# Experts of a fused transformer kernel: three product banks, roots on GpSimd, a last end in halves, and one head fewer inside the causal stage

## The reference

```python
h = x + _gqa(_rmsnorm(x, attn_norm_w), wq, wk, wv, wo)   # causal, 16 heads of 8, 4 key/value heads
out = h + _moe(_rmsnorm(h, ffn_norm_w), gate_w, expert_w)
...
logits = t @ gate_w.T                       # 8 experts
w, sel = jax.lax.top_k(logits, TOP_K)       # TOP_K = 2
w = softmax(w)
for e in range(N_EXPERTS):
    out = out + comb[:, e, None] * (t @ expert_w[e].T)
```

## Time and profile before

| | us |
|---|---|
| median of 3 runs | 719.98 (717.72 to 722.4) |
| the profiled execution | 719.72 |
| its span, first to last instruction | 718.0 |

### The profile page before, as it was taken

The page is one execution under the profiler, slowest core; times in us unless marked ns, Lnnn a source line. Parts: engine busy times, 40 slices in busy tenths (PEclk is TensorE's granted clock), DMA queues, the critical chain, the costliest instruction groups (busy, mean ns, idle before and its releaser), DMA issues. The chain is left out here.

```text
span 718.0 us, 11711 instructions
## 1 busy us (share of the span) xinstructions
PE 559.0 (78%) x3810; PEld 309.0 (43%) x3810; DVE 524.0 (73%) x2256; ACT 367.5 (51%) x748; POOL 250.6 (35%) x414
## 2 busy tenths in 40 slices
PE   1966488478866999589999999999999978868660
PEld 1855487376654664112233333333334533535220
DVE  6699998532564776599899999999981554676883
ACT  5741145301102667004678778888787453655562
POOL 2001118600004568201344444444444443424443
PEclk9987565556986999655899999999999888988895
DMA  8000000000000283300111211112100000000001
GB/s 301 1 1 1 1 1 0 0 1 0 1 1 1 77 252 123 100 0 6 29 35 35 56 34 30 34 34 56 36 1 7 1 1 1 0 0 31 0 29 58
DMA packets 17003, 24.76 MB, mean 34 GB/s; under 512 B 3182, under 2 KB 13950, under 8 KB 16766
## 3 DMA queue, kind: packets, MB, share of 16 engines
q1 hardware_dynamic: 16366, 21.91, 9.9%
q10 hardware_dynamic: 576, 2.10, 0.8%
HBM read 13.65 MB, written 10.35 MB: 33 GB/s over the span
## 5 line engine op out<-in xcount | busy, mean ns | idle before, releaser
L1406 DVE CUSTOM_DVE_ANT_0 d_masked_S<-d_pS,d_wide_mask 128x512 bf16<-128x512 f32 (+3 forms) x512 | 217.0, 485 | 12.1 <-PE d_pS L1548 8.0
L1522 ACT ACTIVATE d_P<-d_pT 128x768 f32<-128x768 f32 (+1 forms) x192 | 166.0, 883 | 62.8 <-PE d_pT L1548 61.9
L1375 POOL TENSOR_SCALAR_AFFINE_SELECT d_P<-d_P 128x256 f32<-128x256 f32 x256 | 103.4, 417 | 174.9 <-ACT d_P L1522 174.9
L1548 PE MATMUL d_pS<-Ks,Qs 48*128 48x512 bf16 (+3 forms) x512 | 111.2, 332 | 23.7 <-DVE d_mx L1406 13.0
L1548 PE MATMUL d_pO<-d_P,V 128*32 128x512 f32 (+3 forms) x1024 | 98.6, 460 | 1.8 <-POOL d_P L1375 1.8
L1548 PE MATMUL d_pT<-Qs,Ks 51*128 51x512 bf16 (+3 forms) x512 | 73.1, 314 | 1.6 <-ACT d_mT L1492 1.6
L1548 PEld LDWEIGHTS d_pS<-Ks,Qs 48*128 48x128 bf16 x512 | 34.9, 97 | 77.3 <-DVE d_mx L1406 67.4
L1548 PEld LDWEIGHTS d_pT<-Qs,Ks 51*128 51x128 bf16 x512 | 20.8, 95 | 74.6 <-ACT d_P L1522 43.2
L1845 PE MATMUL e_PE<-gate_expT,w_qkvT 128*128 128x512 f32 x96 | 48.7, 655 | 4.3 <-PEq L58 2.5
L1406 DVE DVE_READ_ACCUMULATOR2_ANT d_mx<- 128x1 f32 x512 | 42.4, 83 | 0.0
L1548 PEld LDWEIGHTS d_pO<-d_P,V 128*32 128x32 f32 x1024 | 20.8, 109 | 32.9 <-issue 29.6
(11 more groups left out here) (309 smaller groups left out, 1059.2 us busy)
## 6 DMA issues: line engine op xcount, KB each, us to landing
Qs<-q_stack SPq DMA_DIRECT2D x32, 192.0 KB, 3.1
q_stack<-Qp SPq DMA_DIRECT2D x8, 384.0 KB, 2.6
X<-in_x_dram ACTq DMA_DIRECT2D x4, 512.0 KB, 6.1
q_stack<-Qp SPq DMA_DIRECT2D x8, 256.0 KB, 2.5
out_dram<-e_moe SPq DMA_DIRECT2D x4, 512.0 KB, 2.6
w_qkvT<-in_w_qkvT_dram SPq DMA_DIRECT2D x1, 1536.0 KB
Ks<-k_stack SPq DMA_DIRECT2D x32, 48.0 KB, 3.2
q_stack<-Qp SPq DMA_DIRECT2D x8, 128.0 KB, 2.1
```

What stands on the lines that cost most here:

```text
L1375: last = nc.gpsimd.affine_select(out=view, in_=view, compare_op=ALU.is_ge, fill=0.0, base=0, pattern=[[0, 2], [1, 128]], channel_multiplie ...
L1406: last = nc.vector.tensor_tensor_reduce(out=out_[:, at:at + w], in0=src[:, at:at + w], in1=wide_mask[:, 512 - w:512], scale=1.0, scalar=LO ...
L1522: nc.scalar.activation(P[pair % 4][:, :, P_AT[unit]:P_AT[unit] + w], pT[(3 * pair + unit) % 2][:, :, 0:w], ACT.Exp, scale=float(HD4) ** -0 ...
L1548: return nc.tensor.matmul(out, lhsT, rhs, start=start, stop=stop)
```

## The change

Inside the causal stage only chunk 0's head is left (`EARLY` = 1). The heads of chunks 1 to 3 lie in the experts' stage, where the steps now run from eight tiles ahead of a chunk to one ahead. PSUM is shared out anew: one PA tile instead of two, and three product banks instead of two; PE may write tile u once tile u - 3 has been scaled, and waits for the scaled logits of the head before ahead of the next head's transposes. Both roots of the experts' stage (RMS of a head, deviation of a chunk's end) move from ACT and DVE to POOL: a multiply-add and a power of -0.5, with `half_power` kept from the causal stage. POOL's list runs by turns, with each half-add one turn later. The last chunk's end is cut in halves of four tiles: DVE totals the first half at turn 30; after the last product the second half; ACT normalises the first half, DVE the second, DVE adds x to both, and each half has its own store.

```diff
-EARLY = 2
+EARLY = 1
...
-        PA = [ph.ps(f"PA{k}", [128, CT, D]) for k in two]
-        PE_ = [ph.ps(f"PE{k}", [128, NE, D]) for k in two]
+        PA = ph.ps("PA", [128, CT, D])
+        RING = 3
+        PE_ = [ph.ps(f"PE{k}", [128, NE, D]) for k in range(RING)]
+        LAST = CHUNKS - 1
+        HALF = CT // 2
+        scaled = lambda u: (sm["scaled_a" if u % 2 else "scaled_d"], u // 2 + 1)
...
-        PE_STEPS = {-11: "attention_by_channel", -9: "project", -7: "h_by_channel", -5: "gate"}
-        DVE_STEPS = {-8: "residual", -4: "choose", -2: "weigh", 11: "total", 13: "normalise"}
-        ACT_STEPS = {-10: "attention_by_channel", -7: "mean_square", -6: "h_by_channel", -3: "exp_difference",
-                     12: "deviation", 13: "normalise"}
-        TURNS = range(TILES + 6)
+        PE_STEPS = {-8: "attention_by_channel", -7: "project", -5: "h_by_channel", -4: "gate"}
+        DVE_STEPS = {-6: "residual", -3: "choose", -1: "weigh", 6: "total_first", 10: "total", 12: "normalise"}
+        ACT_STEPS = {-8: "attention_by_channel", -6: "mean_square", -5: "h_by_channel", -2: "exp_difference",
+                     12: "normalise"}
+        POOL_STEPS = {-5: "inverse_root", 11: "deviation"}
+        TURNS = range(TILES + 5)
...
+                def inverse_root(c):
+                    pool.wait_ge(sm["sq"], c - EARLY + 1)
+                    nc.gpsimd.tensor_scalar(top.ms[c][:, :], top.sq[c][:, :], 1.0 / D, RMS_EPS, ALU.mult, ALU.add)\
+                        .then_inc(early["ms"], 1)
+                    pool.wait_ge(early["ms"], c + 1)
+                    nc.gpsimd.tensor_tensor(top.rr[c][:, :], top.ms[c][:, :], top.half_power[:, :], ALU.pow)\
+                        .then_inc(early["rrms"], 1)
+
+                def deviation(c):
+                    pool.wait_ge(sm["mv"], c + 2 if c == LAST else c + 1)
...
+                for u in TURNS:
+                    if 1 <= u <= TILES:
+                        sem, count = scaled(u - 1)
+                        pool.wait_ge(sem, count)
+                        product = T[(u - 1) % 4]
+                        nc.gpsimd.tensor_tensor(product[:, 0:NE // 2, :], product[:, 0:NE // 2, :],
+                                                product[:, NE // 2:NE, :], ALU.add).then_inc(sm["halved"], 1)
+                    for step, c in due(u, POOL_STEPS):
...
+                    if u >= CT + 6 and u % CT == 6 and u // CT - 1 < LAST:
                         finish(u // CT - 1)
-                finish(CHUNKS - 1)
...
+                def finish_last():
+
+                    c = LAST
+                    dve.wait_ge(sm["norm"], c + 1)
+                    for t in range(HALF, CT):
+                        last = nc.vector.tensor_scalar(h[c][:, t, :], h[c][:, t, :], rs[c][:, t:t + 1], std[c][:, t:t + 1],
+                                                       ALU.mult, ALU.add)
...
                         if step == "choose":
-                            inverse_root(c)
-                            choose(nc, dve, top, c, PA[c % 2][:, 0, 0:CT * NE].rearrange("p (t e) -> p t e", e=NE))
+                            choose(nc, dve, top, c, PA[:, 0, 0:CT * NE].rearrange("p (t e) -> p t e", e=NE))
...
+                        if step == "total_first" and c == LAST:
+                            total(c, slice(0, HALF), c + 1)
                         if step == "total":
-                            total(c)
+                            total(c, slice(HALF if c == LAST else 0, CT), c + 2 if c == LAST else c + 1)
...
-                    act.wait_ge(sm["sq"], c - EARLY + 1)
-                    nc.scalar.activation(top.ms[c][:, :], top.sq[c][:, :], ACT.Sqrt, scale=1.0 / D, bias=top.eps_rms[:, :])\
-                        .then_inc(sm["rms"], 1)
...
                 def attention_by_channel(c):
-                    tokens_by_channel(nc, top, PA[c % 2], O4[c]).then_inc(early["oT_psum"], 1)
+                    pe.wait_ge(early["scale"], c)
+                    tokens_by_channel(nc, top, PA, O4[c]).then_inc(early["oT_psum"], 1)
...
-                        if u >= 2:
-
-                            pe.wait_ge(sm["scaled_a" if u % 2 else "scaled_d"], u // 2)
+                        if u >= RING:
+
+                            pe.wait_ge(*scaled(u - RING))
```

More of the change, by code:

```diff
@@ L1695, in _ @@
             def _(sp):
-                for c in chunks:
+                for c in chunks[:LAST]:
                     sp.wait_ge(sm["out"], c + 1)
                     sp.dma_start(out[:, CT * c:CT * c + CT, :], moe[c][:, :, :]).then_inc(sm["stored"], 16)
-                sp.wait_ge(sm["stored"], 16 * CHUNKS)
+                for n, half in enumerate((slice(HALF, CT), slice(0, HALF))):
+                    sp.wait_ge(sm["out_last"], n + 1)
+                    at = slice(CT * LAST + half.start, CT * LAST + half.stop)
+                    sp.dma_start(out[:, at, :], moe[LAST][:, half, :]).then_inc(sm["stored"], 16)
+                sp.wait_ge(sm["stored"], 16 * (LAST + 2))
             @block.gpsimd
@@ L1706, in finish @@
                         .then_inc(sm["out"], 1)
[L1708 to L1712, removed]
+                def inverse_root(c):
[7 more added lines that the diff above has]
+                    pool.wait_ge(sm["mv"], c + 2 if c == LAST else c + 1)
+                    nc.gpsimd.tensor_scalar(std[c][:, :], mv[c][:, :, 1], 1.0, LN_EPS, ALU.mult, ALU.add)\
+                        .then_inc(sm["var"], 1)
+                    pool.wait_ge(sm["var"], c + 1)
+                    nc.gpsimd.tensor_tensor(rs[c][:, :], std[c][:, :], top.half_power[:, :], ALU.pow)\
+                        .then_inc(sm["rstd"], 1)
+                for u in TURNS:
[6 more added lines that the diff above has]
+                    for step, c in due(u, POOL_STEPS):
+                        if step == "inverse_root":
+                            inverse_root(c)
+                        if step == "deviation":
+                            deviation(c)
+                    if u >= CT + 6 and u % CT == 6 and u // CT - 1 < LAST:
                         finish(u // CT - 1)
-                finish(CHUNKS - 1)
             @block.vector
@@ L1719, in residual @@
                     dve.wait_ge(early["proj"], c + 1)
[L1720 removed]
+                    nc.vector.tensor_tensor(h[c][:, :, :], PA[:, :, :], h[c][:, :, :], ALU.add)\
                         .then_inc(early["h"], 1)
[L1723 to L1725 removed]
                 def scale_tile(u):
@@ L1740, in sum_tile, with total @@
                                             AX.X, ALU.add).then_inc(sm["summed"], 1)
-                def total(c):
-                    dve.wait_ge(sm["summed"], c * CT + CT)
-                    nc.vector.tensor_tensor(h[c][:, :, :], h[c][:, :, :], moe[c][:, :, :], ALU.add)\
+                def total(c, at, done):
+                    dve.wait_ge(sm["summed"], CT * c + at.stop)
+                    nc.vector.tensor_tensor(h[c][:, at, :], h[c][:, at, :], moe[c][:, at, :], ALU.add)\
                         .then_inc(sm["total"], 1)
-                    dve.wait_ge(sm["total"], c + 1)
-                    for t in range(CT):
+                    dve.wait_ge(sm["total"], done)
+                    for t in range(at.start, at.stop):
                         last = nc.vector.bn_stats(st[c][:, t, :], h[c][:, t, :])
                     last.then_inc(sm["stats"], 1)
-                    dve.wait_ge(sm["stats"], c + 1)
-                    for t in range(CT):
+                    dve.wait_ge(sm["stats"], done)
+                    for t in range(at.start, at.stop):
                         last = nc.vector.bn_aggr(mv[c][:, t, :], st[c][:, t, :])
@@ L1764, in normalise @@
                         .then_inc(sm["norm"], 1)
+                def finish_last():
[4 more added lines that the diff above has]
+                                                       ALU.mult, ALU.add)
+                    last.then_inc(sm["y_last"], 1)
+                    dve.wait_ge(sm["y_last"], 1)
+                    nc.vector.tensor_tensor(moe[c][:, HALF:CT, :], h[c][:, HALF:CT, :], X[c][:, HALF:CT, :], ALU.add)\
+                        .then_inc(sm["out_last"], 1)
+                    dve.wait_ge(sm["y"], c + 1)
+                    nc.vector.tensor_tensor(moe[c][:, 0:HALF, :], h[c][:, 0:HALF, :], X[c][:, 0:HALF, :], ALU.add)\
+                        .then_inc(sm["out_last"], 1)
                 for u in TURNS:
@@ L1824, in _ @@
                         for e in range(NE):
-                            last = nc.scalar.activation(T[u % 4][:, e, :], PE_[1][:, e, :], ACT.Copy,
+                            last = nc.scalar.activation(T[u % 4][:, e, :], PE_[u % RING][:, e, :], ACT.Copy,
                                                         scale=comb[u // CT][:, u % CT, e:e + 1])
@@ L1872, in _ @@
                         if step == "gate":
-                            gate(nc, pe, top, PA[c % 2][:, 0, :], c)
+                            gate(nc, pe, top, PA[:, 0, :], c)
         ph.close()
```

29 lines of the change are left out of this document (12 added, 17 removed).

## The result

The changed kernel takes 726.14 us (median of 7 runs, 723.96 to 726.35) against 718.93 of the kernel before in the same comparison: ratio 1.0094, interval 1.0072 to 1.0116. It is a little slower, by just under 1%; 721.0 had been forecast. The execution whose profile follows took 723.96 us (span 721.9) at a mean granted clock of 0.827 and is the fastest of the seven; the four at 726.1 us and above had 0.821. The profile shows 4.2 of the 7.2 us between the medians; where the other 3.0 fell is in no trace.

What follows compares the result with a forecast made beforehand. PE was taken to bound the causal rest; in the experts' stage no engine was full, with odd tiles or heads' waits setting the pace. Causal -7.2, stage +3.6, clock +4.9 gave +1.3 on 719.7: 721.0 us, range 711 to 730.

Steps and rivals of the forecast that it cites:

- The causal stage: End of causal stage: without chunk 1's head the last group's transposes come sooner, -7.2 us (bounds 5 and 9.0).
- The chain of a head: Experts' stage: head steps waiting in order across engine lists set the chunk length, 30.1 us in chunks 1 and 2.
- the clock term: Experts' stage: tiles after the three gates run slow, 1.5, 2.7 and 2.7 us, less 2.0 given back: +4.9.
- The ring of three banks: Experts' stage products: the odd lane's 4.32 us loop goes, but no bank wait is in the chain; worth nothing by itself.
- the first rival: Experts' stage: heads hide and the banks' pace rules, three banks lifting 4.32 us a pair to 3.44; 704.4 us, chance 0.2.
- The roots: Experts' stage: power on GpSimd takes 2.0 us a root, hidden before the gate in a head, so costs nothing there.
- The last chunk: Last experts' chunk: +0.8 up to the last scaled product, -1.9 at the end; 38.7 us against 39.8.
- the seven powers: GpSimd root powers in the experts' stage: could cost DVE up to 11.8 us through shared interfaces; taken as nothing.
- the second rival: Experts' stage: PE stands in each head and the clock stays low after it, +12 us; 729.3 us, chance 0.23.
- the low-clock case: Whole kernel: clock at 0.50 after every head, 4 us a head, none given back; 729.3 us, chance 0.23.
- the line of 1%: Whole kernel: result forecast within 1% (7.2 us) of the kernel before, chance 0.57; slower 0.23, faster 0.2.

Runs made afterwards that it cites:

- The earlier finish: Changed kernel with GpSimd's finish of a chunk one turn earlier (u % 8 == 5): 723.2 us, against the changed kernel's 726.1.
- wide gate: Changed kernel with the experts' stage gate matmuls multiplying 128 columns instead of 8, the other 120 not read: 719.6 us.
- PE kept busy: Changed kernel in which PE, where it would stand in a head, multiplies the next tile one or three times beforehand: 724.2 us.

## Why the prediction was right, and where it was off

*The causal stage:* -7.2 forecast, -7.2 between the same two marks. The pace of 6.32 us a group (6.28) and 2.5 for the low clock (2.4, from the 8.65 us between the first two groups) were the right steps.

*The chain of a head:* right in its order and its links. PE stood 5.49 and not 5.6 before the transposes of h; the total lay ahead of the residual, and taking it out gave 6.8 us, where its two times 3.5 make 7.0. From the transposes of h to the gate it took 5.4 us in chunk 1, 5.65 were summed; but of the 2.8 that PE was to stand there again only 0.36 and 0.58 came in chunks 1 and 2, since the transposes and tile 12 ran at the low clock (1.97 and 3.31 for 1.09 and 1.88) beside ACT's work. With their shares of the clock term, chunks 0 to 2 were forecast at 30.7, 32.8 and 32.8 and took 32.0, 31.1 and 31.2: the sum is 2.0 us too high, as much as the clock term gave back without naming a chunk.

*The ring of three banks,* "worth nothing by itself here": right, 0.7 us and inside the intervals. This settles the first rival, which needed the pace of the banks to rule and gave 704.4.

*The roots:* the size was right (0.20 + 1.65 us with a gap of 0.08, 2.0 forecast), the cover held in the heads, and in the sum they were right by way of the chain that I added up without table loads. What I had not drawn from it is that the alternative costs 4.2 us.

*The last chunk* is the term that failed: 38.7 forecast, 41.6 measured. The end itself was right (-1.9 forecast, -2.1). The part up to the last scaled product takes 26.5 us and not the 23.5 of the step (22.7 before). It hangs on ACT's normalising of chunk 2. In the kernel before:

```profile
695.58 3.19 ACT L1813 ACTIVATE N<-N,e_std,e_rs 128x128 f32<-128x128 f32 x8 [1.60 <-DVE e_std L1763]
698.68 2.12 ACT L1825 ACTIVATE Qs<-e_PE,comb 128x128 f32<-128x128 f32 x8
```

In the changed kernel, DVE's shift and then ACT:

```profile
698.32 1.19 DVE L1790 TENSOR_TENSOR e_std<-e_std,shift 128x8 f32<-128x8 f32 x1
...
699.54 3.18 ACT L1850 ACTIVATE N<-N,e_std,e_rs 128x128 f32<-128x128 f32 x8 [8.08 <-DVE e_std L1790]
702.63 2.12 ACT L1862 ACTIVATE e_T<-e_PE,comb 128x128 f32<-128x128 f32 x8
```

The normalising begins 19.2 us after the chunk's first tile, where it was 17.4, and two tiles of ACT lie behind it, where it was one: 7.3 us from its start to the last scaled product for 5.2. The step named both (DVE behind, the normalising ahead of the last two tiles) and priced them at 0.8 us together; they make 3.8. Into the later start go the waits of DVE for GpSimd. The prediction had the row for them, an add on DVE which ended after POOL's, and the rule of the Trainium skill on the shared interfaces; it asked only whether the seven powers meet DVE, and took nothing. But the powers weren't what met DVE: the finish and the half-adds, which before had lain at other turns, met the weighing, which took 4.0 to 4.2 us for the 1.5 of before (644.21 to 645.68), and a half-add met the shift (1.19 us for 0.17); ACT stood 3.17 us for the weights of chunk 3. The earlier finish, 2.9 us in the whole, left this stretch as it was, and no run moves the normalising behind the last tiles: that these two make the 3.8 is read from the rows, not shown by a run of its own.

*The clock:* +4.9 forecast, which is 6.9 for the tiles behind the three gates less 2.0. The tiles behind the first and the third gate (the second is shown above):

```profile
609.85 10.03 PE L1880 MATMUL e_PE<-gate_expT,w_qkvT 128*128 128x512 f32 x16
...
673.40 7.09 PE L1880 MATMUL e_PE<-gate_expT,w_qkvT 128*128 128x512 f32 x12
```

From start to start the three stretches take 9.87, 8.64 and (three tiles) 6.94 us, 6.5 more than at 1.72 a tile: the size was right, by other shares. A wide gate alone gives 6.5 in the medians and with PE kept busy 8.9; since the traces show 3.0 of the 6.5, how much of the slow tiles is hidden behind other engines stays open. The mechanism of the second rival was named in part only: "PE stands ... the clock falls". It falls so (0.52 at 634 to 638 in the kernel with the wide gate), but keeping PE busy in it gives 1.9 alone and 2.3 on top of the wide gate. The larger part is the fall behind the gate. The Trainium skill (TensorE: Matmul & The Clock Gate, section HAM oscillation) speaks of gaps in which PE idles; the trace agrees for the standing, while the gate shows the same fall without a gap.

*The whole:* 721.0 forecast with 711 to 730, 726.1 measured. Between the profiled executions +1.3 was forecast and +4.2 came, and the 2.9 are those of the last chunk; the rest of the difference between the medians is in no trace. The whole lies below the low-clock case of 729.3; a part of that case was in it. The interval of the ratio takes in the line of 1%, so that the result fell on the forecast side of that line is partly luck.

## What to carry to other kernels

A step that moves from a stage with slack on its other engines into one where five in-order lists hand it round can cost far more than its share of the busiest engine: here 9 us of PE became 16.8. Before adding buffers, follow the chain with every engine's list in hand, and look at what stands ahead of each step in the list: one turn later for the total was worth 6.8 us, the third bank 0.7. And for each instruction that moves on GpSimd, ask which small VectorE operations it will now meet.

## What the runs showed of the hardware

The granted clock fell to half while PE was full by the profile's count. In the changed kernel PE is busy for 2.00 us of each of the windows from 558 to 564 with the causal stage's gate (matmuls of eight columns, 2.03 us) in the middle, and the clock goes 1.00, 0.78, 0.50. With PE kept busy in the experts' stage, four tiles behind the narrow gate took 7.11 us in the first head and 10.01 in the second, so the fall does not follow every such gate; with 128 columns in the gate as well they took 7.03 in both, and the wider matmuls cost 2.05 us for 1.95.

VectorE operations of eight elements a partition waited for GpSimd's instruction of the moment to end: 0.17 us became 0.95 to 1.19, and a pair of comparisons that takes 0.36 became 3.65. All of these read two tensors from SBUF but the one of L1182 (1.13 us), which has a single tensor input. The Trainium skill (GPSIMD Engine Reference, Key points) names instructions with two SBUF inputs or in a two-port mode. The trace agrees for the first kind; in which mode L1182 ran no run shows. Not every operation waited: a reciprocal of the same size took 0.20 us beside a half-add (651.88), and two sums of one input 2.01 beside the finish (648.79), as when alone.
